# Attention stages of a macaron network: unit order, planning of the maxima, and the place of the output projection

## The chip, the cores and the metric

The kernel runs on one core of a Trainium2 chip. The metric is the device time of one execution in microseconds. Three runs of the kernel before took 4042.51, 4048.62 and 4051.37 us; the median is 4048.62.

## The reference

Input and state `x` have shape (1, 2048, 128), float32. Twelve residual steps follow each other: low-rank feed-forward and wide attention, two mixtures of experts around a long convolution, then the part that matters here:

```python
x = x + 0.5 * _L2_ffn_ref(_layernorm(x), ...)
x = x + _L2_attn_ref(_layernorm(x), ...)        # 16 heads of 8, rotary, full
x = x + 0.5 * _L2_ffn_ref(_layernorm(x), ...)
x = x + 0.5 * _L3_ffn_ref(_layernorm(x), ...)   # full attention with a gate, then experts
x = x + _L3_attn_ref(_layernorm(x), ...)        # rotary, causal
x = x + 0.5 * _L3_ffn_ref(_layernorm(x), ...)   # as above, again

# the ends of _L2_attn_ref (and _L3_attn_ref) and of _L3_ffn_ref's attention:
attn = jax.nn.softmax(scores, axis=-1)
ctx = jnp.einsum('bhqk,bhkd->bhqd', attn, v)    # to (B, T, 128)
return ctx @ Wo + bo

gate = jax.nn.sigmoid(out @ gate_w + gate_b)
attn = out * gate @ out_w
x = _ln(src + attn, n1_g, n1_b)                 # experts follow
```

So there are four attention stages: three full ones (the first ends in a projection with a bias, the other two in a gate and a projection without one) and a causal one, which stands third and ends in a projection with a bias.

## The kernel before, in words

The 2048 tokens are cut into four chunks of 512 (`CH`) or sixteen tiles of 128. The stages follow each other; a stage waits for the `ends` of the one before (`fence`), on each engine. `Prepare` norms the rows, makes queries, keys and values, splits queries and keys into bf16 parts and packs them through DRAM, so that a score product of 64 rows is as exact as a float32 one. Its last work is SP's gathering of 48 DMAs.

`Heads` is the attention itself. A unit is a group of four heads and a chunk of 512 queries: `(g, q)`, 16 units. `HeadsPlan` writes one list of steps; every engine walks it in its order and does its own part, so the list is the order in each engine's queue.

- `max`: TensorE multiplies a tile of 128 queries with a chunk of 512 keys for one head (64 rows of the array; the two heads of a pair lie in the two halves, `par`), into one of three banks (5 to 7, `slot_bank`, taken in turn). VectorE reduces the bank to 128 maxima (`tensor_reduce`, L1874). A full unit has 64 of these, a causal one of chunk k 16(k+1). Where causal tiles lie on the diagonal, a second small product adds the mask.
- `finish` and `rows`: when a unit's maxima are there, VectorE joins them, GpSimd splits them into three bf16 parts (five instructions), TensorE turns them (L1788), ScalarE copies them out (L1853), and SP stores them to DRAM and loads them into the rows of the packed queries (L1747, L1752). The score product then subtracts the maximum by itself.
- `scores` and `exp`: a step proper. TensorE makes the scores of 128 keys by 512 queries for the two heads of a pair, into two of banks 0 to 3 (L1800); ScalarE takes both through the exponential in one instruction (L1840, 128x1024). A full unit has 32 such steps: 16 key tiles by 2 pairs.
- `values`: four matmuls, one for each head, each on a column group of 32 (`tile_position=(0, 32 * hh)`), over 256 of the 512 queries (`part`), into bank 4 (L1815). In the trace a float32 matmul has two records, so a part has eight. Part 0 comes in a tile's first step, part 1 in its second; both wait for the exponentials of the tile before (`waiting`).
- `empty` and `out`: at a unit's end ScalarE copies bank 4 to `EV` (L1860), TensorE turns it by four transposes (L1824), VectorE inverts the sums and writes the unit's columns of the context `CTX` (L1891, L1893).

The planner (`lay_out`) first places all maxima of unit 0, then its row. After that each step gets as many maxima of the units ahead as are needed for unit u+1's to be done `LEAD` = 9 steps before it starts: `n` is the greatest of the quotients of maxima left and steps left, over the deadlines of up to two units ahead. Half of them go before the step's scores and half behind. An item in `later` is run some steps afterwards (`tick`): rows and out 4 steps.

The order of units is group by group, with the chunks up and down: (0,0), (0,1), (0,2), (0,3), (1,3), (1,2) and so on to (3,0). A chunk's context is therefore whole only at the end of the stage, and what follows it stands behind: `ProjectOut` (transposes L631, copies by ScalarE L637 and VectorE L642 in turn, products L661, the additions of product and of bias L1924, L1926) or the first half of `GatedTail` (transposes, gate product, bias L2126, sigmoid L2259, multiplication L2130, transposes, product, addition of the residual L2135, statistics L2139, L2142, then the square root L2262), each for four chunks.

Of the kernel before, what the change touches and what calls it, by code (L numbers as in the profile page):

```python
# [14 lines left out]
P = 128  # L15
# [31 lines left out]
            mqkv=3 * P, mout=P, mgate=P, mgateb=P, mscale=P, n1g=P, n1b=P, n2g=P, n2b=P,  # L47
# [1522 lines left out]
class HeadsPlan:  # L1570
# [5 lines left out]
    LEAD = 9  # L1576

    def __init__(self, causal):
        self.causal = causal
        self.units = [(g, NC - 1 - k if g % 2 else k) for g in range(NG) for k in range(NC)]  # L1580
        self.steps, self.slots, self.tiles, self.exps = [], 0, 0, 0
        self.later = []
        self.exp_of, self.tile_off, self.turned = [], [], []
        self.rows_slot, self.out_slot, self.last_max, self.last_tile = {}, {}, {}, {}
        self.lay_out()

    def slot(self):
        self.slots += 1
        return self.slots - 1

    def maxima(self, u):
        g, k = self.units[u]
        chunks = range(k + 1 if self.causal else NC)
        steps = [(u, pp, qt, kc, par) for pp in range(2) for qt in range(TPC) for kc in chunks for par in (1, 0)]
        if u == 0:
            steps.sort(key=lambda step: step[3])
        return [("max", s, n == len(steps) - 1) for n, s in enumerate(steps)]

    def run(self, step):
        if step[0] == "max":  # L1600
            self.steps.append(("max", *step[1], self.slot()))
            if step[2]:
                u = step[1][0]
                self.last_max[u] = self.slots - 1
                self.steps.append(("finish", u))
                self.later.append([4, ("rows", u)])
        else:
            what, u = step
            (self.rows_slot if what == "rows" else self.out_slot)[u] = self.slot()
            self.steps.append((what, u, self.slots - 1))  # L1610

    def tick(self, everything=False):
        for item in list(self.later):
            item[0] -= 1
            if item[0] <= 0 or everything:
                self.later.remove(item)
                self.run(item[1])

    def keys(self, k):
        return TPC * (k + 1) if self.causal else NT  # L1620

    def score_pair(self, u, j, pp):
# [6 lines left out]
        self.steps += [("scores", u, j, pp, first), ("exp", first, 2, self.exps)]  # L1629
        self.exp_of += [self.exps] * 2  # L1630
        self.exps += 1

    def values(self, u, j, first, last, half):
        self.steps.append(("values", u, j, first, last, half))
        if last and half:
            self.last_tile[u] = first + 3
            self.steps.append(("empty", u))
            self.later.append([4, ("out", u)])

    def lay_out(self):  # L1640
        units = self.units
        for step in self.maxima(0):
            self.run(step)
        self.tick(True)
        starts = [0]
        for _, k in units:
            starts.append(starts[-1] + 2 * self.keys(k))
        pending, reached, queued, total, clock = [], 0, [], 0, 0
        waiting = []
        for u, (g, k) in enumerate(units):  # L1650
            n_keys = self.keys(k)
            for j in range(n_keys):
                first = self.tiles
                for pp in range(2):
# [16 lines left out]
        for half in range(2):  # L1671
            self.values(*waiting[0], half)
        self.tick(True)
        self.tick(True)
        rows = set(self.rows_slot.values())
        n = 0
        for slot in range(self.slots):
            self.turned.append((slot in rows, n))
            n += slot in rows


class Heads(Stage):
# [5 lines left out]
    def __init__(self, chip, before, causal):  # L1688
        super().__init__(chip, before)
        sig = chip.sig  # L1690
        self.causal, self.plan = causal, HeadsPlan(causal)
# [7 lines left out]
        self.emptied_v = sig.claim("slot_emptied_vector", p.slots - n)  # L1699
        self.emptied_s = sig.claim("slot_emptied_scalar", n)  # L1700
        self.top = sig.claim("maxima_joined", n)
        self.split = sig.claim("maxima_split", 5 * n)
        self.m_out = [sig.dma(f"maxima_out{k}", n // 2) for k in range(2)]
        self.m_in = [sig.dma(f"maxima_rows{k}", n) for k in range(2)]
        self.scored = sig.claim("scores_made", p.tiles // 2)
        self.exped = sig.claim("scores_exped", p.exps)
        self.valued = sig.claim("values_added", p.tiles // 4)
# [3 lines left out]
                     self.exped[-1], self.filled[-1], self.valued[-1], self.m_in[0][-1], self.m_in[1][-1]]  # L1711

    def emptied(self, slot):

        turned, n = self.plan.turned[slot]
        return self.emptied_s[n] if turned else self.emptied_v[slot - n]

    def gpsimd(self, e):
        c = self.c
        s = self.split  # L1720
        for u in range(len(self.plan.units)):
            k = u % 2
            e.wait_ge(*self.top[u])
            if u > 1:
                e.wait_ge(*self.filled[self.plan.rows_slot[u - 2]])
# [10 lines left out]
    def sync(self, e):  # L1736
        c = self.c
        QR, _ = packed(c)
        for step in self.plan.steps:
            if step[0] == "rows":  # L1740
                _, u, slot = step
                g, q = self.plan.units[u]
# [6 lines left out]
                rows = c.m_dram[k].rearrange("(a h v q) t -> v a h (q t)", a=SPLIT, h=2, v=2)  # L1749
                for par in range(2):  # L1750
                    first = par * HALF + TERMS
                    e.dma_start(QR[first:first + SPLIT * SLOTS:SLOTS, q, 2 * g:2 * g + 2, :],  # L1752
                                rows[par]).then_inc(self.m_in[k].sem, 16)
# [4 lines left out]
    def tensor(self, e):  # L1758
# [8 lines left out]
        for step in plan.steps:  # L1767
            what = step[0]
            if what in ("max", "rows", "out") and step[-1] > 2:
# [706 lines left out]
```

## Time and profile before

| | |
|---|---|
| median of three runs | 4048.62 us |
| profiled execution: time / span | 4049.78 / 4047.9 us |
| mean granted TensorE clock | 0.921 |
| TensorE busy | 3594.8 us, 89% |
| VectorE busy | 3088.4 us, 76% |
| ScalarE busy | 2272.1 us, 56% |
| GpSimd busy | 138.7 us, 3% |
| chain of waits, the three largest lines | L1874 (maxima) 37%, L1815 (values) 9%, L1780 (products for maxima) 6% |
| first attention, full | maxima from 829.9, last context tile 1513.4, projection done 1522.4 |
| second, full with gate | maxima from 1636, last context tile 2318.5, square root at 2337.5 |
| third, causal | scores from 2615.8, exponentials to about 3083 |
| fourth, full with gate | maxima from 3146 |

Busy time of TensorE is not a measure of how near it is to its limit: matmuls are pipelined and their ends are modelled, while their starts are recorded. How far one start is from the next is the surer number. The granted clock is a share of full speed: 1.00 is 2.4 GHz, 0.50 is 1.2 GHz.

### The profile page before, as it was taken

Reading aid. Unit: us, or ns where it says so; the run is one execution under the profiler, and the core shown is the slowest. Engines: PE = TensorE matmul, PEld = TensorE weight load, DVE = VectorE, ACT = ScalarE, POOL = GpSimd, SP = SyncE. Lnnn points to the kernel's source line nnn. Section 1 sums busy time; section 2 is a strip of 40 time slices with the busy share of each in tenths; the row PEclk is TensorE's granted clock in tenths of the full one; section 3 lists DMA queues with packets and bytes.
Section 4 is the critical chain, followed back from the end, with each engine's and each line's share of the span. In section 5 each row is a group of like instructions: output and inputs, shape, how many; then the busy total and the mean of one; then the engine's idle time right before and its main releaser. Section 6 shows DMA issues by size and latency. Waiting matters only on the chain.

```text
span 4047.9 us, 71976 instructions
## 1 busy us (share of the span) xinstructions
PE 3594.8 (89%) x29276; PEld 1462.3 (36%) x29276; DVE 3088.4 (76%) x6440; ACT 2272.1 (56%) x2630; POOL 138.7 (3%) x371
## 2 busy tenths in 40 slices
PE   5889889779999996799999987599997899999886
PEld 3755756412222223122222263233333122222362
DVE  5255545589999955899999547796875899999547
ACT  2222232228888882388888821157475388888821
POOL 0000000110000000000000000200000000000000
PEclk8889889869999997699999989699998699999988
DMA  0010510120000002200000000400001200000000
GB/s 29 2 50 1 119 38 1 35 86 2 2 2 2 2 2 57 86 2 2 2 2 2 23 1 0 115 2 2 2 2 41 75 2 2 2 2 2 23 1 11
DMA packets 32731, 84.57 MB, mean 21 GB/s; under 512 B 10096, under 2 KB 25232, under 8 KB 26000
## 3 DMA queue, kind: packets, MB, share of 16 engines
q1 hardware_dynamic: 32256, 78.17, 7.2%
q8 instruction: 231, 3.78, 0.4%
q10 hardware_dynamic: 144, 1.79, 0.1%
q14 instruction: 100, 0.82, 0.1%
HBM read 65.24 MB, written 14.70 MB: 20 GB/s over the span
## 4 chain that ended last, share of the span: by engine, by line
DVE 46%; PE 45%; ACT 4%; issue 3%; DMA 2%; SPq 1%; POOL 0%; ACTq 0%; DVEq 0%; POOLq 0%
DVE pm L1874 37%; PE ps L1815 9%; PE ps L1780 6%; PE ps L1800 4%; PE ps L949 3%; PE ps L952 3%; PE ps L2099 3%; PE ps L2075 3%; PE ps L1028 3%; ACT arena L1840 1%; PE ps L1477 1%; PE ps L1212 1%; PE ps L748 1%; DVE XN L293 1%; DVE stat L283 1%
## 5 line engine op out<-in xcount | busy, mean ns | idle before, releaser
L1874 DVE TENSOR_REDUCE pm<-ps 128x1 f32<-128x512 f32 (+2 forms) x3712 | 2214.5, 668 | 140.4 <-PE ps L1780 75.7
L1840 ACT ACTIVATE arena<-ps 128x1024 f32<-128x1024 f32 (+3 forms) x1856 | 1851.8, 1001 | 510.8 <-PE ps L1800 357.9
L1780 PE MATMUL ps<-arena 64*128 64x512 bf16 (+2 forms) x3712 | 1298.5, 396 | 29.1 <-DVE pm L1874 15.4
L1815 PE MATMUL ps<-arena,VA 128*16 128x256 f32 (+1 forms) x14592 | 1138.5, 384 | 40.4 <-ACT EV L1860 22.9
L1800 PE MATMUL ps<-arena 64*128 64x512 bf16 (+1 forms) x3712 | 1043.7, 379 | 21.5 <-DMA arena<-m_dram 20.7
L1780 PEld LDWEIGHTS ps<-arena 64*128 64x128 bf16 x3712 | 330.5, 93 | 1081.6 <-DVE pm L1874 894.9
L1815 PEld LDWEIGHTS ps<-arena,VA 128*16 128x16 f32 x14592 | 240.5, 94 | 511.0 <-ACT arena L1840 404.0
L1800 PEld LDWEIGHTS ps<-arena 64*128 64x128 bf16 x3712 | 195.7, 94 | 122.8 <-issue 78.6
L968 ACT ACTIVATE EV<-ps 128x512 f32<-128x512 f32 x128 | 76.3, 597 | 203.0 <-PE ps L949 203.0
L980 DVE TENSOR_TENSOR arena<-EV,ps 128x512 f32<-128x512 f32 x128 | 87.9, 687 | 124.8 <-PE ps L952 120.3
L949 PE MATMUL ps<-XNT,arena 128*128 128x512 f32 x304 | 160.7, 611 | 2.3 <-DVE arena L1255 1.5
L952 PE MATMUL ps<-XNT,arena 128*128 128x512 f32 x304 | 158.5, 603 | 0.0
L319 PE MATMUL ps<-IDF,XN 128*128 128x128 f32 x176 | 51.5, 448 | 101.5 <-DVE XN L293 100.7
L2099 PE MATMUL ps<-arena,EV 128*128 128x512 f32 x256 | 123.1, 625 | 15.7 <-ACT EV L2287 15.7
L1891 DVE RECIPROCAL rd<-ps 128x16 f32<-128x16 f32 x64 | 16.0, 250 | 152.4 <-PE ps L1824 152.3
L1028 PEld LDWEIGHTS ps<-arena 128*128 128x128 f32 x1024 | 115.3, 192 | 2.9 <-issue 2.9
L1028 PE MATMUL ps<-arena 128*128 128x128 f32 x1024 | 115.3, 275 | 0.0
L1477 PE MATMUL ps<-early,XNT 128*128 128x384 f32 x128 | 68.1, 675 | 49.5 <-DVE arena L1509 27.3
L1082 DVE SCALAR_TENSOR_TENSOR X<-ps,prob,X 128x128 f32<-128x128 f32 x256 | 89.8, 351 | 29.1 <-PE ps L1028 22.0
L1726 POOL TENSOR_SCALAR neg<-mx 128x16 f32<-128x16 f32 x64 | 16.1, 252 | 2304.3 <-DVE mx L1883 2304.3
L1853 ACT ACTIVATE mt<-ps 48x128 bf16<-48x128 bf16 x64 | 16.5, 258 | 134.7 <-PE ps L1788 134.7
L952 PEld LDWEIGHTS ps<-XNT,arena 128*128 128x128 f32 x304 | 59.0, 194 | 75.5 <-issue 74.5
(270 smaller groups left out, 2680.3 us busy)
## 6 DMA issues: line engine op xcount, KB each, us to landing
arena<-parts_dram SPq DMA_DIRECT2D x192, 128.0 KB, 2.9
parts_dram<-parts SPq DMA_DIRECT2D x32, 384.0 KB, 2.9
arena<-k_dram SPq DMA_DIRECT2D x20, 528.0 KB, 11.4
arena<-in_pad SPq DMA_DIRECT2D x16, 512.0 KB, 8.0
parts<-k_dram SPq DMA_DIRECT2D x8, 528.0 KB, 6.6
arena<-in_w SPq DMA_DIRECT2D x4, 1024.0 KB, 6.2
early<-in_late SPq DMA_DIRECT2D x1, 2184.5 KB, 8.9
VA<-k_dram SPq DMA_DIRECT2D x4, 528.0 KB, 7.7
```

Of the source, the lines that this page charges most:

```text
L949: e.matmul(c.bank(b), self.first(j), rhs, start=True, stop=True).then_inc(self.gate.sem, 1)
L952: e.matmul(c.bank(2 + b), self.second(j), rhs, start=True, stop=True).then_inc(self.up.sem, 1)
L1028: ins = e.matmul(c.bank(4 + g % 4)[:, q * P:(q + 1) * P], self.HT[(k - 1) % 2][:, 2 * ex + s, tt * P:(tt + 1) * P], w3[:, 2 * ex + s, :], ...
L1082: e.scalar_tensor_tensor(c.X[:, i, :], c.bank(4 + g % 4)[:, (ex % 4) * P:(ex % 4 + 1) * P], c.prob[:, i, ex:ex + 1], c.X[:, i, :], ALU.mul ...
L1477: e.matmul(c.bank(2 + i % 2)[:, 0:3 * P], c.XNT[:, i * P:(i + 1) * P], self.weights, start=True, stop=True).then_inc(self.projected.sem, 1)
L1780: ins = e.matmul(bank[:, 0:w], QR[half(par), q, 2 * g + pp, qt * P:(qt + 1) * P], KT[half(par), kc, 2 * g + pp, 0:w], start=True, stop=not ...
L1800: ins = e.matmul(c.bank((t + par) % 4)[:, off:CH], KT[half(par), j // TPC, 2 * g + pp, j % TPC * P:(j % TPC + 1) * P], QR[half(par), q, 2 ...
L1815: ins = e.matmul(c.bank(4)[32 * hh:32 * hh + VW, a:b], c.VA[:, j, GH * g + hh, :], self.PB[:, (first + hh) % self.PBS, a:b], start=j == 0 ...
L1840: e.activation(self.PB[:, s:s + 2, offs[0]:CH], c.bank(t % 4, 2).rearrange("p (a t) -> p a t", a=2)[:, :, offs[0]:CH], ACT.Exp, scale=self ...
L1874: e.tensor_reduce(c.pm[:, u % 2, at, kc:kc + 1], self.slot_bank(slot)[:, 0:w], AX, ALU.max).then_inc(self.emptied_v.sem, 1)
L2075: ins = e.matmul(c.bank(2 + h)[:, 0:H1], self.masks[k % 2][:, ex, at:at + P], self.w1[:, ex * H1:(ex + 1) * H1], start=False, stop=ex == E ...
L2099: ins = e.matmul(c.bank(2 + 2 * k + half), self.HTt[k][:, s * P:(s + 1) * P], self.w2[:, s, half * CH:(half + 1) * CH], start=s == 0, stop ...
```

## The change

1. The units' order becomes chunk by chunk: for each chunk its four groups. Full stages take the chunks 0, 1, 2, 3, the causal one 0, 3, 2, 1.
2. The last unit becomes two, one for each pair of heads; each has half the maxima and half the steps, and both parts of a values product (with two matmuls each) in one step.
3. 14 maxima of unit 1 (`AHEAD`) are placed before the first step, and unit 0's row after the first four of them (`EARLY`).
4. `ProjectOut` and the gate's part of `GatedTail` go. Two classes, `Project` and `Gate`, hold the work on one chunk, and the plan places it as steps that use the three banks of the maxima: `turn` 3 steps after the chunk's last `out`, then `gate` and `project` each 3 later. All four chunks are treated so; the last one's work comes at the stage's end, one after the other.
5. The bias of the projection is added to `X` by GpSimd at the stage's start. The gate works on turned data: one matmul of 512 columns, the sigmoid with the bias as a column, a multiplication by GpSimd, and a product that turns back by itself. The second set of transposes goes. `mgateb` becomes one column.

```diff
-    LEAD = 9
+    LEAD, EARLY, AHEAD = 9, 4, 14
+    SCALAR = ("rows", "turn", "gate")
-        self.units = [(g, NC - 1 - k if g % 2 else k) for g in range(NG) for k in range(NC)]
+        self.order = (0, 3, 2, 1) if causal else (0, 1, 2, 3)
+        self.units = [(g, k, (0, 1)) for k in self.order for g in range(NG)]
+        g, k, _ = self.units.pop()
+        self.units += [(g, k, (0,)), (g, k, (1,))]
...
+        self.place(what, *where)
+        if what == "out":
+            g, k, pairs = self.units[where[0]]
+            if g == NG - 1 and pairs[-1] == 1:
+                self.later.append([3, (self.behind[0], (k,), None)])
+        elif what in self.behind[:-1]:
+            self.later.append([3, (self.behind[self.behind.index(what) + 1], where, None)])
...
         for step in self.maxima(0):
             self.run(step)
+        pending, reached, queued, total, clock = self.maxima(1), 1, [], 0, 0
+        queued.append((starts[1] - self.LEAD, len(pending)))
+        for n in range(min(self.AHEAD, len(pending) - 1)):
+            if n == self.EARLY:
+                self.tick(True)
+            self.run(pending.pop(0))
+            total += 1
         self.tick(True)
...
                     if waiting:
-                        self.values(*waiting[0], pp)
+                        for part in range(2) if len(pairs) == 1 else (n_pair,):
+                            self.values(*waiting[0], part)
...
-                for hh in range(GH if a < b else 0):
+                for n in range(n_heads if a < b else 0):
+                    hh = 2 * pairs[0] + n
                     ins = e.matmul(c.bank(4)[32 * hh:32 * hh + VW, a:b], c.VA[:, j, GH * g + hh, :],
-                                   self.PB[:, (first + hh) % self.PBS, a:b], start=j == 0 and part == 0, stop=last,
+                                   self.PB[:, (first + n) % self.PBS, a:b], start=j == 0 and part == 0, stop=last,
                                    tile_position=(0, 32 * hh), skip_group_check=True)
...
+class Project:
+    KINDS = ("turn", "project")
...
+    def gpsimd_first(self, e):
+        for k in range(NC):
+            if k:
+                e.wait_ge(*self.biased[k - 1])
+            e.tensor_tensor(self.xs(k), self.xs(k), bc(self.bias, TPC), ALU.add).then_inc(self.biased.sem, 1)
...
+    def turn(self, e, heads, k, bank):
+        c = self.c
+        e.wait_ge(*heads.ready(k))
+        for t in range(TPC):
+            ins = e.transpose(bank[:, t * P:(t + 1) * P], c.CTX[:, TPC * k + t, :], c.IDF[:, :])
+        return ins
...
+    def scalar(self, e, heads, what, k, bank):
+        return e.activation(self.chunk(k), bank, ACT.Copy)
+    def vector(self, e, heads, what, k, bank):
+        e.wait_ge(*self.biased[k])
+        return e.tensor_tensor(self.xs(k), tiles(bank), self.xs(k), ALU.add)
+class Gate(Project):
+    KINDS = ("turn", "gate", "project")
...
+    def gpsimd(self, e, heads, what, k):
+        if what == "gate":
+            n = heads.plan.order.index(k)
+            e.wait_ge(*heads.emptied(heads.plan.slot_of["gate", k]))
+            e.tensor_tensor(self.sg(k), self.sg(k), self.chunk(k), ALU.mult).then_inc(self.gated.sem, 1)
+    def tensor(self, e, heads, what, k, bank):
+        if what == "turn":
+            return self.turn(e, heads, k, bank)
+        if what == "gate":
+            e.wait_ge(*heads.emptied(heads.plan.slot_of["turn", k]))
+            return e.matmul(bank, self.gate, self.chunk(k), start=True, stop=True)
+        e.wait_ge(*self.gated[heads.plan.order.index(k)])
+        for t in range(TPC):
+            ins = e.matmul(bank[:, t * P:(t + 1) * P], self.sg(k)[:, t * P:(t + 1) * P], self.weights, start=True,
+                           stop=True)
+        return ins
+    def scalar(self, e, heads, what, k, bank):
+        if what == "turn":
+            return e.activation(self.chunk(k), bank, ACT.Copy)
+        return e.activation(self.sg(k), bank, ACT.Sigmoid, bias=self.bias)
...
-        then(Heads, False)
-        then(ProjectOut, chip.ep("wo2"), chip.ep("bo2"))
+        then(Heads, False, Project(chip, chip.ep("wo2"), chip.ep("bo2")))
```

## Rows read from the trace of the kernel before

**Rows 1.** Groups of one shape, second stage (1636 to 2318 us): busy, mean ns, idle.
```profile
L1874 DVE TENSOR_REDUCE pm<-ps 128x1 f32<-128x512 f32 x1024 | 619.0, 681 | 8.7 <-PE ps L1780 7.3
```

**Rows 2.** Busy by stretch (length; PE, PEld, DVE, ACT, POOL busy), clock, DMA.
```profile
876.00:886.00 10.00, 10.00 (x50) 1.89 (x47) 8.65 (x14) 4.92 (x5) 0.00 (x0) 0.52 0.01 2
1300.00:1350.00 50.00, 49.25 (x497) 13.72 (x489) 49.80 (x86) 42.31 (x44) 1.62 (x8) 1.00 0.01 2
1470.00:1510.00 40.00, 35.01 (x384) 8.94 (x382) 0.55 (x2) 37.22 (x40) 0.00 (x0) 1.00 0.01 2
...
2860.00:2880.00 20.00, 19.03 (x115) 5.48 (x108) 14.47 (x28) 6.23 (x10) 1.08 (x5) 0.66 0.01 2
...
3040.00:3060.00 20.00, 20.00 (x202) 6.84 (x203) 8.98 (x18) 14.03 (x18) 1.08 (x5) 1.00 0.01 2
```

**Rows 3.** Chain of waits, one unit apart: start, us, what.
```profile
1368.02 20.37 DVE pm L1874 x34
...
1407.43 4.82 DVE pm L1874 x8
```

**Rows 4.** Timeline after unit 0's maxima: start, us, instructions [idle before <-releaser].
```profile
868.33 0.22 DVE L1883 TENSOR_REDUCE mx<-pm 128x16 f32<-128x64 f32 x1
...
870.86 0.34 SPq L1747 DMA_DIRECT2D m_dram<-mt  x1
...
875.16 0.61 PE L1800 MATMUL ps<-arena 64*128 64x512 bf16 x2 [4.18 <-DMA arena<-m_dram]
...
876.23 4.88 DVE L1874 TENSOR_REDUCE pm<-ps 128x1 f32<-128x512 f32 x8 [4.52 <-PE ps L1780]
```

**Rows 5.** Timeline, TensorE, steps with one maximum each, causal stage.
```profile
2773.97 0.39 PE L1800 MATMUL ps<-arena 64*128 64x512 bf16 x2
...
2775.07 0.39 PE L1800 MATMUL ps<-arena 64*128 64x512 bf16 x2
```

**Rows 6.** Timeline, the first stage's last values products.
```profile
1508.75 0.39 PE L1800 MATMUL ps<-arena 64*128 64x512 bf16 x2
1509.07 0.63 PE L1815 MATMUL ps<-arena,VA 128*16 128x256 f32 x8
1510.26 1.06 PE L1815 MATMUL ps<-arena,VA 128*16 128x256 f32 x16 [0.56 <-ACT arena L1840]
```

**Rows 7.** Timeline, TensorE, float32 products over the whole array, feed-forward.
```profile
1539.16 1.02 PE L949 MATMUL ps<-XNT,arena 128*128 128x512 f32 x2
1540.01 1.02 PE L952 MATMUL ps<-XNT,arena 128*128 128x512 f32 x2
```

**Rows 8.** Timeline, the exit of the first stage.
```profile
1513.09 0.29 DVE L1893 TENSOR_TENSOR CTX<-ps,rd 128x128 f32<-128x128 f32 x1
...
1514.21 0.60 ACT L637 ACTIVATE XNT<-ps 128x512 f32<-128x512 f32 x1 [2.22 <-PE ps L631]
...
1519.16 1.13 PE L661 MATMUL ps<-early,XNT 128*128 128x128 f32 x8 [0.20 <-DVE X L1924]
...
1521.71 0.69 DVE L1926 TENSOR_TENSOR X<-X,early 128x512 f32<-128x512 f32 x1
```

**Rows 9.** Timeline, the exit of the second stage, up to the square root.
```profile
2318.17 0.29 DVE L1893 TENSOR_TENSOR CTX<-ps,rd 128x128 f32<-128x128 f32 x1
...
2337.51 0.31 ACT L2262 ACTIVATE sd<-mv,eps 128x16 f32<-128x16 f32 x1 [7.25 <-DVE mv L2142]
```

**Rows 10.** Timeline, ScalarE, a change to the sigmoid's table.
```profile
1601.31 1.28 ACT L1417 ACT_TABLE_LOAD   x1
1602.61 0.26 ACT L1417 ACTIVATE CTX<-CTX 128x64 f32<-128x64 f32 x1
```

**Rows 11.** Timeline, GpSimd on a chunk beside VectorE's first maxima.
```profile
829.94 38.36 DVE L1874 TENSOR_REDUCE pm<-ps 128x1 f32<-128x512 f32 x64
829.98 1.15 POOL L1465 TENSOR_TENSOR parts<-arena,parts 128x512 bf16<-128x512 f32 x1 [2.71 <-ACT parts L1549]
```

**Rows 12.** Timeline, the causal stage's first row of maxima and scores.
```profile
2610.46 0.58 SPq L1747 DMA_DIRECT2D m_dram<-mt  x1
...
2615.76 0.61 PE L1800 MATMUL ps<-arena 64*128 64x512 bf16 x2 [8.16 <-DMA arena<-m_dram]
```

More of the change, by code:

```diff
@@ L1628, in score_pair, with values @@
         self.tile_off += [off, off]
[L1629 to L1636, printed above, removed]
+        self.steps += [("scores", u, j, pp, first), ("exp", first)]
+        self.exp_of += [first // 2] * 2
+    def values(self, u, j, first, last, part):
+        self.steps.append(("values", u, j, first, last, part))
+        if part:
+            self.value_of += [self.n_values] * (2 * len(self.units[u][2]))
+            self.n_values += 1
+        if last and part:
+            self.last_value[u] = self.n_values - 1
             self.steps.append(("empty", u))
-            self.later.append([4, ("out", u)])
+            self.later.append([4, ("out", (u,), None)])
     def lay_out(self):
@@ L1720, in gpsimd @@
         s = self.split
-        for u in range(len(self.plan.units)):
+        self.behind.gpsimd_first(e)
+        for step in self.plan.steps:
+            if step[0] in self.behind.KINDS:
+                self.behind.gpsimd(e, self, step[0], step[1])
+            if step[0] != "finish":
+                continue
+            u = step[1]
             k = u % 2
@@ L1768, in tensor @@
             what = step[0]
-            if what in ("max", "rows", "out") and step[-1] > 2:
+            if what in ("max", "rows", "out") + self.behind.KINDS and step[-1] > 2:
                 e.wait_ge(*self.emptied(step[-1] - 3))
@@ L1826, in tensor @@
                 ins.then_inc(self.filled.sem, 1)
+            elif what in self.behind.KINDS:
+                self.behind.tensor(e, self, what, step[1], self.slot_bank(step[2])).then_inc(self.filled.sem, 1)
     def scalar(self, e):
@@ new lines, in vector @@
+                    c.CTX[:, TPC * q:TPC * q + TPC, at].rearrange("p q (h d) -> p q h d", d=HD),
+                    bank.rearrange("p (q h w) -> p q h w", q=TPC, h=GH)[:, :, heads, 0:HD],
+                    bcl(c.rd[:, :].rearrange("p (q h) -> p q h", q=TPC)[:, :, heads], HD),
+                    ALU.mult).then_inc(self.emptied_v.sem, 1)
+            elif what in self.behind.KINDS and what not in plan.SCALAR:
+                e.wait_ge(*self.filled[step[2]])
+                self.behind.vector(e, self, what, step[1], self.slot_bank(step[2])).then_inc(self.emptied_v.sem, 1)
@@ L2037, in tensor @@
         self.fence(e)
-        self.turn.tensor(e)
-        self.gate.tensor(e)
-        self.turn_gated.tensor(e, lambda i: e.wait_ge(*self.gated[i // TPC]))
-        self.product.tensor(e)
         for k in range(NC):
```

258 lines of the change are left out of this document (118 added, 140 removed).

## The prediction

> **What bounds the kernel now.** I read first the page's engine rows, then the stretches, then single steps of the four attention stages, which hold some 2,500 of the 4,048 us. A stage is a list of steps; a step is one pair of score tiles, its exponential and half of a values product, while VectorE works off maxima for the units to come. The three full stages have 512 steps and 1,024 maxima each (16 units of 32 steps and 64 maxima) [rows 1]. In their middle VectorE is busy 49.8 of 50 us, ScalarE 42.3 [rows 2]: the chain runs along the maxima, and a unit takes 39.41 us (1407.43 less 1368.02) [rows 3], 1.232 us a step, 0.616 us a maximum. TensorE is close behind: a full step with one maximum repeats after 1.10 us (2775.07 less 2773.97) [rows 5], so with two it has at most a tenth to spare.
>
> VectorE is not the bound at three places. After unit 0's maxima it waits from 868.5 to 876.2 for the row of maxima to pass GpSimd, TensorE, ScalarE and two DMAs [rows 4]. In the next 10 us TensorE runs at a granted 0.52, near its lower level, and only 14 VectorE instructions and 5 exponentials get done [rows 2]. And in the last 43 us of the stage it has nothing left: from 1470 to 1510 ScalarE runs 38 exponentials and two copies [rows 2], 1.06 us a step. The causal stage is bound by TensorE (20.0 of 20 us at 3040, VectorE 9.0) [rows 2].
>
> **1. Ends of stages.** Before, the four chunks' turning, product and bias stand after the last context tile: 1513.38 to 1522.40, 9.0 us [rows 8]. Afterwards only the last chunk is left: turning up to the copy's start 0.8, copy 0.65, four matmuls 1.15, addition 0.7, waits 0.1: 3.4. Saves 5.6, in two stages (the bias goes to GpSimd, under unit 0's maxima). With the gate the stretch up to the square root is 2318.46 to 2337.51, 19.05 us [rows 9]; afterwards turning and copy 1.45, gate product 1.3, sigmoid 0.65, GpSimd's multiplication 1.15 [rows 11] to 1.7 (taken: 1.5), four matmuls and addition 1.95, sixteen statistics 4.3: 11.2. Saves 7.8, twice. Together -26.8. The weights that SP loads behind this fence start some 8 us later against the last context tile, but are wanted only 45 us further on. SP gets three more DMAs for the extra unit and is else unchanged.
>
> **2. Second unit's maxima early.** Fourteen maxima fill the hole of [rows 4]; four of them cover GpSimd's splitting, so TensorE waits for nothing. They are worth at most 14 x 0.6 = 8.4 us of VectorE. The first scores slip by up to 0.8 us (TensorE must issue all fourteen first), and in the 10 us at low clock the order of the steps stays as it was. By 886 VectorE then stands at 26 instead of 15 maxima of unit 1: 11 x 0.6 = 6.6. Bounds 4 and 8.4. Three stages: -19.8. In the causal stage the hole ends when SP, busy until 2610.46 with the gathering, gets to the row [rows 12]: nothing, both ways.
>
> **3. Last unit halved, the costly edit.** The planner's rates, worked: before, two maxima a step to step 471, none in the last 41. Afterwards nine steps with one (439 to 448), sixteen with two, sixteen with one up to 480, then 32 steps of halves, seven of them with one. The halves have two heads. A values product is four matmuls side by side on four column groups of 32; each streams 256 columns. Eight records (one part) take 0.63 and sixteen (two parts) 1.06 [rows 6]: 0.43 a part. A whole-array f32 product of 512 columns takes 0.85 (1540.01 less 1539.16) [rows 7], just the same rate. So the time hangs on columns, not on how many groups run, and two heads cost what four do. A half's step does both parts: 0.43 x 2, 0.11 until the next can start, and scores 0.32 (1509.07 less 1508.75) [rows 6] = 1.29 us, TensorE's, against 1.06 ScalarE's now; with one maximum 1.51.
> Before, from step 439: 32 x 1.232 + 41 x 1.06 = 82.9. After: 25 x 1.10 + 16 x 1.23 + 7 x 1.51 + 25 x 1.29 = 90.0, and one more unit's transposes, row and drained bank on a TensorE without slack, 2.4: 92.4. Cost +9.5, three times +28.5. Bounds: if two heads took half the time, a half's step would be ScalarE's again and the cost 1.5; above, 12. In the causal stage the last unit has eight key tiles, four of them cut by the diagonal: its extra values are 4 x 0.86 + 2.15 = 5.6, and 1.4 for the unit: +7.
>
> **4. A chunk's work between tiles.** Three chunks of four are done inside. Without a gate: VectorE 0.69 for the addition, four transposes and four matmuls on TensorE (0.65 and 1.1). VectorE is at most three banks behind, and one bank is lent to the insertion; I take 1.0 a chunk, +3.0 in the first stage (2 to 6).
> With the gate ScalarE must change its table and back: a load is 1.28 us and the next function starts 0.02 after it [rows 10]. Twice 1.28 and the sigmoid 0.63 make a hole of 3.2 us in the exponentials. Behind the waiting ScalarE stand the next exponentials; the values two steps on wait for them, and TensorE's queue behind those holds the maxima. VectorE has about 1.5 us in its banks; with 0.56 for the delayed values product it idles some 2.2 us. Turning 0.1, projection 0.9: 3.2 a chunk, 9.6 a stage, +19.2 in two (6 if the slack of 7.7 in 50 us of ScalarE swallowed it, 30 if nothing did).
> The Trainium skill (ScalarE: Activation LUTs, "What ACT_TABLE_LOAD costs") puts a switch at about 2.66 us, load plus a drain of about 1.38. The trace shows the 1.28 but no drain behind or before it. By the page the six gates' holes would be 2.8 us longer each, +17 us: an estimate from its figure.
> GpSimd's multiplication stands ahead of a later unit's splitting, 13 steps off: nothing. Beside 64 maxima GpSimd's 1.15 us cost VectorE nothing [rows 11]: their 38.36 us is 0.6 each.
>
> **5. Order of causal units.** Four units of the smallest chunk come first, then the largest. The planner then asks for unit 4's 64 maxima in seven steps, nine a step: 35 us of VectorE beside some 22 of TensorE, 13 lost. Won back: the small units in the middle, where TensorE's clock sank once (0.66 at 2860, ten ScalarE instructions in 20 us) [rows 2], about 8 to 10. Net +4.5, bounds -8 and +18. The three insertions cost a TensorE without slack 1.8 each: +5. With the halving +16.5 in this stage.
>
> **Sum:** -26.8 - 19.8 + 28.5 + 3 + 19.2 + 16.5 = +20.6 us. The profiled execution took 4049.8 (span 4047.9), so it becomes 4070.4; it stands 1.2 above the median of the runs shown, 4048.6, and on that footing the forecast is 4069.
>
> **Rivals.**
> A, two-headed values run in half the time. For it: ends of matmuls are modelled in the profile. Against: the starts, which are not, agree with a whole-array product. Then the halving costs 1.5 x 3 + 1.5: 27 + 2 less, 4039, faster. The point is a half's step under 1.06 us.
> B, ScalarE's change of tables costs twice its 1.28 us, since here it stands in the midst of exponentials that take both pairs of banks in turn: 6 gates x 2 loads x 1.28 = 15, so 4084. It decides from the point where VectorE's banks are empty. Against: no gap stands at the load shown [rows 10]. The Trainium skill's rule named above points this way.
> C, insertions hide in TensorE's and ScalarE's slack: VectorE's additions alone stay (9 x 0.69), 22 becomes 8: 4055. For it: ScalarE's 7 us slack per 50. Against: banks hold only 1.8 us.
> D, the causal order wins instead (-8): 4057, and with C 4043. For it: VectorE and TensorE each lose some time at 2600 and 2840 now.
>
> **How the numbers follow.** This kernel can be told from no change beyond 0.2%, 8 us. Forecast 0.42, B 0.11, A 0.18, C 0.14, D 0.08, C or A joined with D 0.07. Slower by over 8 us: the forecast's, B's and a few of D's, 0.55. Within: C and D, 0.20. Faster: A and joined cases, 0.25. Range: 4032 to 4090; the forecast's own 4056 to 4082.
>
> **What would show it.** In the full stages: VectorE without a hole after unit 0 (part 2); in the last 32 steps exponentials 1.29 us apart with TensorE ahead of them (part 3; 1.03 to 1.06 would be A); holes in VectorE of about 2 us at each gate (4); exits of 3.4 and 11.2 us (1); in the causal stage nine maxima to a step early on, and the stage longer by some 11 us net of its exit (5). The forecast is wrong if the full stages get shorter by more than their exits.

## The result and the profile after

The changed kernel takes **4092.1 us** (median of four runs, 4090.7 to 4097.1) against 4050.0 for the kernel before beside it (four runs, 4042.5 to 4060.2): ratio 1.0105, 95% interval 1.008 to 1.0129. It is slower, as forecast, but by 42 us and not by 20.6, and 2 us above the range of 4032 to 4090. The profiled execution took 4090.7 (span 4088.7), 40.9 more than that of before. Where they lie:

| stage: first maxima's start to last exponential's start | before | after | difference | forecast |
|---|---|---|---|---|
| first, full | 679.25 | 686.76 | +7.5 | +5.9 |
| second, full with gate | 678.20 | 692.95 | +14.8 | +12.5 |
| third, causal | 496.43 | 526.79 | **+30.4** | +16.5 |
| fourth, full with gate | 678.84 | 693.20 | +14.4 | +12.5 |

That is 67.1 more where the forecast had 47.4. The exits give 21.5 back where it had 26.8. Another 3.7 are gained ahead of the first stage, where nothing was changed (its first maxima start at 826.2 instead of 829.9; in the runs below they start anywhere from 825.9 to 830.7), and about 1.0 elsewhere between the stages.

Lines of the changed kernel are 1912 for VectorE's maxima (1817 their products), 1837 scores, 1880 exponentials, 1854 values; in the kernels of the experiments they lie a few lines off. The timeline after unit 0 in the first stage, VectorE (start, us, instructions, idle before): the hole of [rows 4] is gone.

```profile
864.59 0.22 DVE L1921 TENSOR_REDUCE mx<-pm 128x16 f32<-128x64 f32 x1
864.73 14.03 DVE L1912 TENSOR_REDUCE pm<-ps 128x1 f32<-128x512 f32 x23
879.18 1.29 DVE L1912 TENSOR_REDUCE pm<-ps 128x1 f32<-128x512 f32 x2 [0.42 <-PE ps L1817]
```

The halves of the last unit in the first stage: exponentials start 1.29 us apart (1488.50, 1489.79), and so do scores (1488.07, 1489.36), as forecast; the two values parts of two heads take 1.04, as [rows 6] has 1.06 for two parts of four heads. TensorE ends the chain and ScalarE waits 0.27 a step.

```profile
1488.07 0.39 PE L1837 MATMUL ps<-arena 64*128 64x512 bf16 x2
1488.38 0.55 PEld L1854 LDWEIGHTS ps<-arena,VA 128*16 128x16 f32 x8 [0.23 <-ACT arena L1880]
1488.38 1.04 PE L1854 MATMUL ps<-arena,VA 128*16 128x256 f32 x8
1488.50 1.02 ACT L1880 ACTIVATE arena<-ps 128x1024 f32<-128x1024 f32 x1 [0.27 <-PE ps L1837]
1489.36 0.10 PEld L1837 LDWEIGHTS ps<-arena 64*128 64x128 bf16 x2 [0.42 <-issue]
...
1489.79 1.02 ACT L1880 ACTIVATE arena<-ps 128x1024 f32<-128x1024 f32 x1 [0.27 <-PE ps L1837]
```

The exit of the first stage, against [rows 8]: from the context tile's end at 1517.04 to 1520.46 are 3.4 us, as forecast.

```profile
1516.82 0.22 DVE L1933 TENSOR_TENSOR CTX<-ps,rd 128x64 f32<-128x64 f32 x1
...
1517.86 0.60 ACT L1985 ACTIVATE XNT<-ps 128x512 f32<-128x512 f32 x1 [2.14 <-PE ps L1972]
...
1519.77 0.69 DVE L1989 TENSOR_TENSOR X<-ps,X 128x512 f32<-128x512 f32 x1 [2.72 <-PE ps L1980]
```

The exit of the second stage, against [rows 9], takes 14.3 us to the square root (2345.63 less 2331.36), not 11.2. Two things were not in the sum: the gate's matmul and the four of the projection take 2.05 each, where they take 1.13 and 1.16 inside the stage, since the granted clock fell to its lower level at 2332.7, while TensorE waited for ScalarE's copy; and the table for the square root is loaded after the last statistics, 1.28 in plain sight (before, it was loaded in the shade, 8.5 us ahead of its use). In the fourth stage the level held until 3882.4, and the exit takes 12.6 (19.06 before): 11.2, the load, and little more.

```profile
2332.92 2.05 PE L2021 MATMUL ps<-XNT,early 128*128 128x512 f32 x2 [0.78 <-ACT XNT L2030]
2335.00 0.69 ACT L2031 ACTIVATE parts<-ps,early 128x512 f32<-128x512 f32 x1 [0.93 <-PE ps L2021]
2335.77 1.26 POOL L2014 TENSOR_TENSOR parts<-parts,XNT 128x512 f32<-128x512 f32 x1 [39.79 <-ACT parts L2031]
...
2337.17 2.05 PE L2024 MATMUL ps<-early,parts 128*128 128x128 f32 x8 [2.21 <-POOL parts L2014]
2339.26 0.69 DVE L2035 TENSOR_TENSOR CTX<-ps,XN 128x512 f32<-128x512 f32 x1 [7.89 <-PE ps L2024]
...
2344.34 1.28 ACT L2338 ACT_TABLE_LOAD   x1 [8.65 <-DVE mv L2224]
2345.63 0.31 ACT L2338 ACTIVATE sd<-mv,eps 128x16 f32<-128x16 f32 x1
```

The causal stage is where the difference is. Busy time by stretch (length; PE, PEld, DVE, ACT, POOL busy with counts; granted clock, DMA share, GB/s), first of the kernel before:

```profile
2600.00:2640.00 40.00, 29.93 (x135) 8.81 (x134) 27.64 (x54) 6.15 (x9) 1.08 (x5) 0.54 0.22 61
2640.00:2680.00 40.00, 37.56 (x309) 12.43 (x309) 38.44 (x72) 20.40 (x26) 1.08 (x5) 1.00 0.01 2
2680.00:2720.00 40.00, 39.05 (x369) 12.20 (x370) 36.05 (x66) 26.81 (x32) 1.08 (x5) 1.00 0.01 2
```

and of the changed one, the same stretches and the next:

```profile
2600.00:2640.00 40.00, 30.96 (x135) 9.95 (x134) 18.08 (x39) 6.69 (x10) 2.85 (x11) 0.50 0.35 103
2640.00:2680.00 40.00, 38.52 (x185) 11.10 (x184) 23.58 (x47) 10.99 (x17) 2.17 (x10) 0.50 0.01 2
2680.00:2720.00 40.00, 38.84 (x181) 9.84 (x181) 30.73 (x55) 7.91 (x12) 1.08 (x5) 0.50 0.01 1
2720.00:2760.00 40.00, 39.34 (x348) 12.43 (x345) 32.97 (x60) 26.11 (x29) 0.42 (x2) 0.89 0.01 2
```

Read the granted clock first. Before, TensorE is back at 2.4 GHz (1.00) at 2636.7. Afterwards it stays at 1.2 GHz (0.50) until 2728.7. From 2680 to 2720, where the forecast saw VectorE as the bound with nine maxima a step, VectorE is busy 30.7 of 40 and TensorE 38.8, doing 181 matmuls where it did 369. But this stretch is a mixture. The 64 maxima of the first large unit run from 2664.2 to 2706.8, and there VectorE is busy 37.5 of 43 us and TensorE 40.4:

```profile
2664.00:2707.00 43.00, 40.36 (x165) 10.25 (x162) 37.50 (x67) 6.46 (x10) 0.41 (x2) 0.50 0.00 1
```

So the steep demand does come, and it nearly fills VectorE: even with a TensorE at full clock this part could be shorter by some 5 us only (43 less 37.5, an estimate).

### The profile page after: what moved, and what is told of

Same layout as the page of the kernel before. It is cut to its first block, busy times and chain, and to the rows that moved or that the text cites. A ratio compares the mean times of both kernels' runs of the same rounds, so it can differ in the third digit from the quotient of the medians.

```text
span 4088.7 us, 71978 instructions
## 1 busy us (share of the span) xinstructions
PE 3674.0 (90%) x29216; PEld 1474.9 (36%) x29216; DVE 3086.0 (75%) x6416; ACT 2298.2 (56%) x2654; POOL 163.1 (4%) x407
## 4 chain that ended last, share of the span: by engine, by line
PE 47%; DVE 45%; issue 3%; ACT 3%; DMA 1%; SPq 1%; POOL 0%; POOLq 0%; ACTq 0%; DVEq 0%
DVE pm L1912 37%; PE ps L1854 10%; PE ps L1817 6%; PE ps L1837 4%; PE ps L949 3%; PE ps L952 3%; PE ps L2196 3%; PE ps L2172 3%; PE ps L1028 3%; PE ps L1477 1%; PE ps L1212 1%; PE ps L748 1%; PE ps L1820 1%; DVE XN L293 1%; PE ps L1841 1%
## 5 line engine op out<-in xcount | busy, mean ns | idle before, releaser
L1912 DVE TENSOR_REDUCE pm<-ps 128x1 f32<-128x512 f32 (+1 forms) x3712 | 2233.9, 672 | 195.4 <-PE ps L1817 113.1
L1880 ACT ACTIVATE arena<-ps 128x1024 f32<-128x1024 f32 (+2 forms) x1856 | 1857.9, 1002 | 539.8 <-PE ps L1837 358.5
L1817 PE MATMUL ps<-arena 64*128 64x512 bf16 (+1 forms) x3712 | 1317.5, 401 | 18.2 <-DVE arena L1521 11.0
L1854 PE MATMUL ps<-arena,VA 128*16 128x256 f32 (+1 forms) x14592 | 1189.9, 385 | 29.3 <-ACT EV L1895 25.4
L1837 PE MATMUL ps<-arena 64*128 64x512 bf16 (+2 forms) x3712 | 1041.3, 381 | 13.8 <-DMA arena<-m_dram 8.5
L1854 PEld LDWEIGHTS ps<-arena,VA 128*16 128x16 f32 x14592 | 262.6, 94 | 555.8 <-ACT arena L1880 398.8
L1477 PE MATMUL ps<-early,XNT 128*128 128x384 f32 x128 | 70.1, 691 | 46.9 <-DVE arena L1509 25.8
```

The lines of the kernel that those rows point to most:

```text
L1477: e.matmul(c.bank(2 + i % 2)[:, 0:3 * P], c.XNT[:, i * P:(i + 1) * P], self.weights, start=True, stop=True).then_inc(self.projected.sem, 1)
L1817: ins = e.matmul(bank[:, 0:w], QR[half(par), q, 2 * g + pp, qt * P:(qt + 1) * P], KT[half(par), kc, 2 * g + pp, 0:w], start=True, stop=not ...
L1837: ins = e.matmul(c.bank((t + par) % 4)[:, off:CH], KT[half(par), j // TPC, 2 * g + pp, j % TPC * P:(j % TPC + 1) * P], QR[half(par), q, 2 ...
L1854: ins = e.matmul(c.bank(4)[32 * hh:32 * hh + VW, a:b], c.VA[:, j, GH * g + hh, :], self.PB[:, (first + n) % self.PBS, a:b], start=j == 0 a ...
L1880: e.activation(self.PB[:, s:s + 2, off:CH], c.bank(t % 4, 2).rearrange("p (a t) -> p a t", a=2)[:, :, off:CH], ACT.Exp, scale=self.scale). ...
L1912: e.tensor_reduce(c.pm[:, u % 2, at, kc:kc + 1], self.slot_bank(slot)[:, 0:w], AX, ALU.max).then_inc(self.emptied_v.sem, 1)
```

## The experiments

Each is the changed kernel with the edit shown, if nothing else is said; times are medians. The kernel before, run beside them, had medians of 4057.2 (the first four), 4052.2 (the filling, order 0, 1, 2, 3, projections last, the first version) and 4056.5 (the others), single runs from 4041.8 to 4065.0. So differences between medians of different groups are uncertain by some us. The length of a stage comes from one profiled execution of each kernel; where kernels share the plan of a full stage it agrees within 0.7 us, of the causal stage within 1.5.

**No halves.**

```diff
-        g, k, _ = self.units.pop()
-        self.units += [(g, k, (0,)), (g, k, (1,))]
```

> The changed kernel without the halving of the last unit, all four attention stages. Theory of the forecast (a two-headed values part costs what a four-headed one does): the last 32 steps go back from 1.29 us to about 1.06 each, a full stage gets shorter by 9.5 to 10.4, the causal one by 7: 3 x 10 + 7 = 37, so about 4055 us. Rival A (two heads take half the time): 3 x 1.5 + 1.5 = 6 shorter, about 4086.

Measured 4054.6 (ten runs, 4047.3 to 4061.4), 37.5 less. The full stages get shorter by 10.2, 9.2 and 9.0, the causal one by 13.0. Rival A is out. In the first stage exponentials follow each other from 1489.58 without a wait, 1.03 us apart:

```profile
1489.58 11.35 ACT L1878 ACTIVATE arena<-ps 128x1024 f32<-128x1024 f32 x11
```

**The causal stage in the order of before.**

```diff
         self.units = [(g, k, (0, 1)) for k in self.order for g in range(NG)]
+        if causal:
+            self.units = [(g, NC - 1 - k if g % 2 else k, (0, 1)) for g in range(NG) for k in range(NC)]
```

> The changed kernel with the causal stage's units in the order of the kernel before (four heads at a time, chunks up and down: one small unit first, and a small unit is the halved one); all else as changed. Theory (the lost time of this stage is TensorE's clock, which stays at its lower level for 150 us after the start where it stayed 65 before): the first stretch at the lower level ends near 2640 again, and the stage goes from 526.8 back to about 503 (496.4 before, 5 for three insertions, 2 for the halves of a small unit): 23 less, about 4069. Rival (the forecast's own ledger: 13 us lost to maxima on VectorE, 8 to 10 won back in the middle, 7 for halves): 10 less, about 4082, with the lower level no shorter than now or without weight.

Measured 4070.8 (4061.9 to 4075.6). The stage takes 498.3 instead of 526.8, insertions and halves included, and the lower level ends at 2639.6. The same stretches as above:

```profile
2600.00:2640.00 40.00, 31.43 (x125) 9.09 (x124) 28.06 (x56) 6.10 (x8) 2.53 (x11) 0.51 0.36 107
2640.00:2680.00 40.00, 37.78 (x306) 12.52 (x306) 38.56 (x72) 19.31 (x25) 1.09 (x5) 1.00 0.01 2
```

**The gate without another table.**

```diff
-            e.tensor_tensor(self.sg(k), self.sg(k), self.chunk(k), ALU.mult)...
+            e.tensor_scalar(self.sg(k), self.sg(k), 0.5, 0.5, ALU.mult, ALU.add)...
+            e.tensor_tensor(self.sg(k), self.sg(k), self.chunk(k), ALU.mult)...
-        return e.activation(self.sg(k), bank, ACT.Sigmoid, bias=self.bias)
+        return e.activation(self.sg(k), bank, ACT.Tanh, bias=self.half_bias, scale=0.5)
```

> The changed kernel with the gate's sigmoid written as 0.5 + 0.5 tanh(x/2), so that ScalarE needs no other table than the exponentials', and one more GpSimd operation per chunk. Theory (two loads of 1.28 us in the midst of the exponentials make most of the 3.85 us that a gate's chunk costs): no table loads stand beside the gate, a chunk costs about 2.0, 6 x 1.85 = 11 less, and the additional GpSimd operation adds 1.2 to each of two exits: 9 less, about 4083. Rival (the price is the lent bank and the values product's place, not the loads): at most 2 less, plus 2.4 at the exits, about 4092. Rival B (a change of tables costs a drain besides its load): 17 less or more, below 4077.

Measured 4089.2 (4083.1 to 4091.0). The gated stages get 4.1 and 2.9 shorter: the two loads cost 1.0 to 1.4 of a chunk's price. The whole kernel gains 2.9 where the theory had 9 and the rival about nothing. Here is the timeline of a chunk of the changed kernel, where a unit's chain of maxima takes 43.26 us (1835.35 to 1878.61) against 39.41 in [rows 3], so 3.85 for the chunk:

```profile
1855.79 1.13 PE L2021 MATMUL ps<-XNT,early 128*128 128x512 f32 x2
1856.78 1.28 ACT L2031 ACT_TABLE_LOAD   x1
...
1857.83 3.30 DVE L1912 TENSOR_REDUCE pm<-ps 128x1 f32<-128x512 f32 x5 [0.90 <-PE ps L1817]
1857.94 0.62 PE L1854 MATMUL ps<-arena,VA 128*16 128x256 f32 x8
1858.07 0.69 ACT L2031 ACTIVATE parts<-ps,early 128x512 f32<-128x512 f32 x1
1858.78 1.28 ACT L1880 ACT_TABLE_LOAD   x1
...
1860.07 2.85 ACT L1880 ACTIVATE arena<-ps 128x1024 f32<-128x1024 f32 x3
...
1861.15 0.39 PE L1837 MATMUL ps<-arena 64*128 64x512 bf16 x2 [0.86 <-ACT arena L1880]
...
1861.68 1.16 PE L2024 MATMUL ps<-early,parts 128*128 128x128 f32 x8
1861.79 0.69 DVE L1912 TENSOR_REDUCE pm<-ps 128x1 f32<-128x512 f32 x1 [0.67 <-PE ps L1817]
```

and the same place by tanh:

```profile
1859.35 1.12 PE L2026 MATMUL ps<-XNT,early 128*128 128x512 f32 x2
...
1860.51 0.69 ACT L2037 ACTIVATE parts<-ps,small 128x512 f32<-128x512 f32 x1 [0.19 <-PE ps L2026]
...
1861.38 3.68 DVE L1912 TENSOR_REDUCE pm<-ps 128x1 f32<-128x512 f32 x6 [0.90 <-PE ps L1817]
```

The loads' hole stalls TensorE 0.86 and VectorE 0.67 at 1861. VectorE's longest wait, 0.90, stands behind the gate's matmul and is the same with the loads and without. What is left of the price, 2.5 to 2.9, is about TensorE's own added work: 0.65 + 1.13 + 1.16 = 2.9 us on an engine with a tenth to spare. Without a gate that work is 1.8 and the chunk costs 1.54 (a chain of 40.95, 1027.96 to 1068.91); the chain of waits there runs over the transposes (0.66) and the projection (1.16). No run takes this work away by itself, so that it makes the rest of the price is argued from these sizes and that chain.

**No maxima ahead.** `LEAD, EARLY, AHEAD = 9, 4, 0`

> The changed kernel with none of the second unit's maxima ahead of the first scores (AHEAD 0), all else as changed. Theory: VectorE's hole of some 8 us after unit 0 is back, 7.2 us in each of three full stages, nothing in the causal one: 21 more, about 4113. Rival (VectorE isn't what bounds the first units, so the maxima begun early are given back by the time the stage ends): under 8 more, below 4100.

Measured 4117.2 (4111.3 to 4119.7): 25 more; the full stages are 7.3, 9.0 and 6.9 longer, the causal one 1.7 shorter.

**Filling TensorE's wait.**

```diff
             elif what == "scores":
+                if self.causal and t == 0:
+                    for n in range(28):
+                        e.matmul(c.bank(n % 4), KT[half(n % 2), 0, 0, 0:P], KT[half(n % 2), 0, 0, :], ...)
```

> The changed kernel with 28 matmuls of 512 columns, whose results nobody reads, in the 8.5 us in which TensorE waits for unit 0's row of maxima in the causal stage; order and planning stay. They cost at most 2 us. If TensorE's lower level itself makes the causal stage longer and the filling raises it by 2650 instead of 2729, the five units of the start run at twice the rate of TensorE until VectorE's nine maxima a step bound them: 20 to 25 us less, about 4070. If VectorE is the bound there (the forecast's 13 us), the level rises and under 8 us are gained. If the level doesn't rise, nothing changes, 4092 to 4094, and the run settles nothing.

Measured 4090.4 (4088.8 to 4095.8). The level rose for 6.8 us at 2615.9 and fell again at 2622.7, 1 us after the first scores; it came back at 2728.5 as without the filling, and the stage took 526.6. The added matmuls filled 4.7 us of the wait, and 4.2 were left:

```profile
2612.75 4.72 PE L1834 MATMUL ps<-arena 64*128 64x512 bf16 x28
2621.69 0.39 PE L1840 MATMUL ps<-arena 64*128 64x512 bf16 x2 [4.21 <-DMA arena<-m_dram]
```

Inconclusive, as said ahead.

**Three more orders.** `self.order` of the causal stage:

> The changed kernel with the causal stage's chunks in the order 0, 1, 2, 3. The theory (small units with 4 maxima a step at most and then more and more work for TensorE): the maxima of the next size never have to be caught up within seven steps of the smallest unit in a ratio of four to one, but of two to one (32 maxima in 8 steps). The start at the lower level ends by some 2680, half of the excess of 85 us: 12 less, and the last unit halved is the largest, 16 key tiles instead of 8: 4 more. About 4084. If the lost time were the long queue of maxima on VectorE, all 13 would be back: 4083 less 4 given back, so the two differ in the trace alone: by the level between 2640 and 2730.

> The changed kernel with the causal stage's chunks in the order 3, 0, 2, 1: four large units first, then the four smallest, then the steep demand for maxima (48 in seven steps). Theory (the loss is TensorE's lower level during many small units at the start, not the steep demand itself): the level rises before 2660 as in the kernel before, some 12 us later than there because unit 0 now waits for all four chunks of keys; the small units in the middle lower it again for 20 us at most; the stage takes 500 to 512 instead of 526.8: about 4072. Rival (the forecast's 13 us of VectorE behind a steep demand): they are still there, 10 to 12 of them, and the later start is added: 525 to 535, 4090 or above.

> The changed kernel with the causal stage's chunks in the order 3, 2, 1, 0: no unit asks for more maxima than the one before it, the small ones stand last, and the smallest is halved. Theory: lower level until 2650 only, and again for a part of the small units at the end; the stage takes about 505 (8 to 12 for the later start, 5 for insertions, 498 otherwise less the smaller halves): about 4068. Rival (many small units cost the same wherever they stand, by their transposes, rows and drained bank): 520 or more, 4085.

Measured 4092.3 (4077.7 to 4095.9), 4105.6 (4103.7 to 4107.0) and 4083.3 (4080.7 to 4083.6). The stages, with the time that each spent at the lower level:

| causal order | stage | at 1.2 GHz within it |
|---|---|---|
| 3, 2, 1, 0 | 490.9 | 54.9 |
| before (heads first) | 496.4 | 63.1 |
| heads first, with all else changed | 498.3 | 59.4 |
| 3, 0, 2, 1 | 513.7 | 99.3 |
| 0, 3, 2, 1, no halves | 513.8 | 110.6 |
| 0, 3, 2, 1 (the change) | 526.8 | 134.5 |
| 0, 1, 2, 3 | 527.7 | 120.9 |

A line through the seven has 0.44 us of stage per us at the lower level; a bounding TensorE loses 0.5 by half speed. Order 0, 1, 2, 3 never asks for nine maxima a step, and is as long as the change, with TensorE busy all the time at 1.2 GHz and VectorE about half of it:

```profile
2640.00:2680.00 40.00, 40.00 (x216) 11.91 (x212) 20.63 (x42) 11.79 (x18) 2.16 (x10) 0.50 0.01 2
2680.00:2720.00 40.00, 40.00 (x235) 11.17 (x231) 23.75 (x46) 13.94 (x20) 1.08 (x5) 0.54 0.01 1
```

So a stage as long as this comes about without the steep demand (though the halved unit is the largest there, for which I had put 4). What the steep demand adds in the change itself, where it nearly fills VectorE for 43 us, no run separates. In 3, 0, 2, 1, which has such a demand (48 maxima in seven steps), the stage is 13 us shorter than the change, between what theory (500 to 512) and rival (525 to 535) had. Its four small units stand in the middle, and the level falls there for 44.4 us, from 2866.8:

```profile
2840.00:2880.00 40.00, 38.21 (x269) 14.62 (x268) 29.59 (x60) 13.60 (x21) 2.18 (x10) 0.84 0.01 2
2880.00:2920.00 40.00, 39.35 (x239) 11.85 (x238) 28.64 (x53) 14.31 (x21) 1.09 (x5) 0.61 0.01 2
```

All three totals missed: 0, 1, 2, 3 by 8, since the level came back at 2716.7 and not at 2680; the two that begin with chunk 3 by 34 and 15, mainly since their first maxima start 26.5 us later (2620.6 and 2620.8 against 2594.2), the first unit needing all chunks of keys; I had put 8 to 12. The lengths in the table don't hold this delay. By the time of the whole kernel the order of before (4070.8, halves included) beats all four others.

**All projections last.**

```diff
-                self.later.append([3, (self.behind[0], (k,), None)])
+                self.full.append(k)
...
+        for k in self.full:
+            self.later.append([3, (self.behind[0], (k,), None)])
+        self.tick(True)
```

> The changed kernel with all four chunks' turning, gate and projection behind the last unit instead of between tiles; bias on GpSimd, gate transposed, all else as changed. Theory: the stages lose their insertions (1.54 a chunk without gate, 3.85 with one, some 1.8 in the causal stage: 4.6 + 2 x 11.5 + 5.4 = 33 less), the exits get longer (without gate from 3.4 to about 7, with gate from 11 to about 17, four GpSimd multiplications after each other among them): 7.2 + 12 = 19 more. About 4078: the interleaving costs more than it hides. Rival (the insertions' prices are those of one more unit's work wherever it stands, TensorE being without slack): no shorter, 4092 or above.

Measured 4068.9 (4059.8 to 4075.0), 9 less than the theory's 4078, which had 19 for the exits. The stages get shorter by 4.8, 10.4, 2.4 and 10.6. The exits get longer by 10.0 in all: by 2.2 in the first stage (5.6, from 1516.00 to 1521.63, instead of 3.4) and 1.3 in the causal one, by 2.4 in the second (16.7 to the square root instead of 14.3) and 4.1 in the fourth (16.7 instead of 12.6). Of each pair the smaller difference is where the exit of the changed kernel ran partly at the lower level. Four sigmoids share one table load there:

```profile
2320.81 2.06 ACT L2033 ACTIVATE XNT<-ps 128x512 f32<-128x512 f32 x4 [1.25 <-PE ps L1975]
2322.90 1.28 ACT L2034 ACT_TABLE_LOAD   x1
2324.19 2.59 ACT L2034 ACTIVATE parts<-ps,early 128x512 f32<-128x512 f32 x4
```

**Maxima ahead alone, in the kernel before.**

```diff
-        self.tick(True)
...
-        pending, reached, queued, total, clock = [], 0, [], 0, 0
+        pending, reached, queued, total, clock = self.maxima(1), 1, [], 0, 0
+        queued.append((starts[1] - self.LEAD, len(pending)))
+        for n in range(min(14, len(pending) - 1)):
+            if n == 4:
+                self.tick(True)
+            self.run(pending.pop(0))
+            total += 1
+        self.tick(True)
```

> The kernel before with one edit: fourteen of the second unit's maxima ahead of the first scores. Theory (the forecast's second term, as measured in the changed kernel by taking it back: 7.3, 9.0, 6.9 in the full stages, nothing in the causal one): 20 to 23 us less than the kernel before, ratio 0.9945 to 0.995. Rival (the gain hangs on the other edits, since in the kernel before the last 41 steps are free of maxima anyway and VectorE can catch up): under 8 us, ratio 0.998 or above.

Measured 4026.0 (4025.4 to 4029.3), ratio 0.9929 (0.9912 to 0.9946). That is 30.5 below the median beside it, more than the 20 to 23 expected; the profiled executions differ by 23.8, and the stages are 7.3, 6.4, 2.5 and 6.7 shorter, 22.9 in all.

**Two versions made of these.** No halves, the causal order of before, gate by tanh:

> Three edits together: no unit halved, the causal stage's units in the order of the kernel before, the gate by tanh. From what each did alone in its stage: 3 x 9.4 for the halves in the full stages, 13 + 16 in the causal one (526.8 to about 497), 7 for the gates less 2.4 at their exits: 62 less, about 4030 us, faster than both kernels. Rival (the gains of the causal order and of no halving are the same gain in the causal stage, and a disturbed clock takes the rest): 4045 or above.

Measured 4027.0 (4025.2 to 4032.4), ratio 0.9939 (0.992 to 0.9959). And with all projections last, by sigmoid:

> Three edits to the changed kernel: no unit halved, the causal stage's units in the order of the kernel before, and turning, gate and projection of all chunks behind the last unit (gate by sigmoid, one change of tables). From the stages measured: full stages 676.6 - 4.8, 683.8 - 10.4 and 684.2 - 10.6, causal 496 - 2.4, exits 5.6 without gate (2.2 more than with only one chunk left) and 15.3 with it (1.7 more than by tanh): 14 less than the tanh version's 4027, about 4013 us, ratio to the kernel before 0.990. Rival (exits grow by as much as the stages shrink): 4025 or above.

Measured **4011.5** (4010.4 to 4014.8), ratio 0.9893 (0.9876 to 0.991), faster than both kernels. Against the kernel before it holds the maxima begun early, the bias on GpSimd and the gate computed transposed; it has neither halves, nor work between tiles, nor another order of the causal stage. In the full stages, where all units are of one size, the order is still chunk by chunk.

## Why the prediction was wrong

- **1, exits: -26.8 forecast, -21.5 measured.** Without gate 5.6 came in the first stage and 4.7 in the causal one, where the lower level began at 3124.6, inside the exit. With it 6.4 and 4.8 came instead of 7.8 each: the square root's table (1.28), and in the second stage the lower level (two products of 2.05 instead of 1.15).
- **2, maxima ahead: -19.8 forecast, right within 3.4.** Taken back it costs 23.2 in the three full stages. Alone in the kernel before it gives 20.4 there, and 2.5 in the causal stage, where I had nothing. I read the hole of [rows 4] as one wait from 868.5 to 876.2; VectorE does one maximum in it, at 871.01, and is idle 2.46 + 4.52 us.
- **3, halves: +35.5 forecast, +41.4 measured** (28.4 in the full stages against 28.5). The mechanism and its size held: two heads cost what four do. In the causal stage 13.0 instead of 7: with the halves it spends 24 us more at the lower level.
- **4, work between tiles: +22.2 forecast for the three full stages, +25.8 measured** (4.8, 10.4, 10.6, what the kernel with all projections last takes away), and 2.4 instead of 5 in the causal one. The size was near, the reason half wrong, and part of the nearness is luck: I charged ScalarE's hole, and of the 3.5 us that a chunk costs the loads turned out to be 1.0 to 1.4. The rest is most likely TensorE's 2.9 us of added work. The rule of the Trainium skill (ScalarE: Activation LUTs, "What ACT_TABLE_LOAD costs") of a drain of about 1.38 us per switch would have made the two loads dearer than that. The rows of the chunk show no such drain: the load at 1856.78 starts 0.03 us after an exponential has ended, the sigmoid starts 0.01 after its load, at 1858.07, and the exponential 0.01 after the next. Rival B is out.
- **5, the causal order: the step that failed.** The ledger was 13 us lost to VectorE, 8 to 10 won back, +4.5 net. Measured, the order alone costs 17.9: without halves the stage takes 495.9 in the order of before (the first of the two versions above, whose gate by tanh isn't in this stage) and 513.8 in the new one, and TensorE spends 45 us more at 1.2 GHz (110.6 against 65.7). With the 13.0 of the halves and -0.5 for insertions and maxima ahead together this is the 30.4 of the table. In the change as a whole TensorE is at 1.2 GHz for 71 us more of this stage (134.5 against 63.1), a cost that my ledger had at nothing. I had the clue in [rows 2]: in the middle of the stage before, small units had brought the clock to 0.66. I read it as time to be won by moving them, and did not ask what four of them would do at the start, where the granted clock is 0.50 when they begin. Neither of the two bounds, -8 and +18, was worked out from a clock.

That small units at the start go with a long stretch at the lower level, and in the middle with a short one, and that the stage's length follows it, is shown by five orders in seven kernels. That the level alone makes the time is not: the one try to raise it with the order left as it is (the filling) raised it for 6.8 us only. One more observation points the same way. With nothing changed at all, a kernel's time moves with its mean granted clock: the kernel before ran from 4041.8 us at 0.922 to 4065.0 at 0.915, order 0, 1, 2, 3 from 4077.7 at 0.917 to 4095.9 at 0.911. Worked out from these figures that is 0.38 and 0.35 us for each us more at the lower level, an estimate; which of the two moves the other it doesn't say.

Rivals C and D are out too: the insertions did not hide, and the order lost.

## What to carry to other kernels

Before units are reordered, look at the granted clock of the stretch that they are moved into: small units moved to where TensorE is at its lower level were followed by 71 us more of it in this stage. Work put between tiles cost 1.6 us a chunk where it adds 1.8 to the nearly full TensorE, and 3.5 where it adds 2.9 and two table loads: what it adds to the fullest engine tells more than the stall that looks worst in the timeline; at the end of a stage, four chunks together cost 1.3 to 4.1 us more than the last alone. And filling a hole of the bounding engine with its own later work (the maxima begun early) pays about in full, 6.4 to 7.3 us in each full stage for a hole of 7.0 us idle, and needs none of the rest. Last, a stretch of fixed length can hold two phases with different bounds: cut it where the work changes before you read who is full.

## What was not expected of the hardware

The same two products took 2.05 us each at an exit where TensorE had waited 0.8 us ahead of the first and 2.2 ahead of the second, against 1.13 and 1.16 in the stage. With 28 more matmuls (4.7 us) in a wait of 8.5 us the clock rose for 6.8 us and fell again, and stayed low while TensorE's rows show it busy for 38.45 of the 40 us from 2640; in the order 0, 1, 2, 3 it stayed at 0.50 there with all 40.0 of 40 busy. And by tanh, exponentials and gate ran without any table load (4 loads before exponentials in the whole run instead of 10).
